# State space: the closing addition of the soft-plus goes from VectorE to ScalarE and GpSimd

## The reference, cut to what matters

```python
dt = jax.nn.softplus(jnp.einsum('blr,rd->bld', dt_r, W_dt) + b_dt)
A = -jnp.exp(A_log)
def step(h, inp):
    dt_t, B_t, C_t, u_t = inp
    dA = jnp.exp(dt_t[:, :, None] * A)
    h = h * dA + dt_t[:, :, None] * B_t[:, None, :] * u_t[:, :, None]
    y = jnp.einsum('bdn,bn->bd', h, C_t)
    return (h, y)
```

## Time and profile before

| what | us |
|---|---|
| median of 3 runs | 1926.7 |
| the profiled execution, first to last instruction (span) | 1948.6 |
| VectorE busy in the span | 1491.3 (77%) |
| TensorE busy | 1562.9 (80%) |
| ScalarE busy | 953.5 (49%) |
| GpSimd busy | 920.7 (47%) |
| state space, from 700 to 1290 us of the span | 590 |
| VectorE busy there | 540.35 |
| GpSimd busy there | 410.72 |
| ScalarE busy there | 365.03 |
| TensorE busy there | 469.73 |

### The profile page before, as it was taken

How to read it: one execution, slowest core, us unless ns; L and a number is a source line. 1 busy time by engine, 2 the same in 40 slices (tenths; PEclk the granted TensorE clock), 3 DMA queues, 4 the chain that set the end, 5 groups by cost and what they waited for, 6 DMA issues and landing times. The chain is left out here.

```text
span 1948.6 us, 31799 instructions
## 1 busy us (share of the span) xinstructions
PE 1562.9 (80%) x10219; PEld 1017.4 (52%) x10219; DVE 1491.3 (77%) x2947; ACT 953.5 (49%) x1491; POOL 920.7 (47%) x938
## 2 busy tenths in 40 slices
PE   8889888989699978977878878769998811699991
PEld 4545547988476632322333333236776611588891
DVE  6899986887488779999989999967777678533335
ACT  3545543575544567657656666436566410011114
POOL 4455442444200147677676677654344100366653
PEclk8999998999899989999988999979999855799996
DMA  4000000000000000000000000020000040466654
GB/s 144 2 0 0 0 1 27 2 2 1 12 1 0 1 1 1 1 1 0 0 1 0 0 0 1 1 78 11 5 9 5 3 145 0 159 209 206 212 171 135
DMA packets 49075, 75.34 MB, mean 39 GB/s; under 512 B 8861, under 2 KB 34821, under 8 KB 48437
## 3 DMA queue, kind: packets, MB, share of 16 engines
q1 hardware_dynamic: 43541, 64.12, 10.5%
q0 software_dynamic: 4544, 9.32, 1.6%
q10 hardware_dynamic: 864, 0.33, 0.1%
HBM read 62.26 MB, written 11.48 MB: 38 GB/s over the span
## 5 line engine op out<-in xcount | busy, mean ns | idle before, releaser
L1506 POOL TENSOR_TENSOR m_hC<-m_h,m_Cs 128x512 f32<-128x512 f32 x256 | 328.2, 1287 | 169.2 <-DVE m_h L1680 122.6
L1788 PE MATMUL PS<-m_hC,identf 128*128 128x512 f32 x512 | 296.5, 662 | 100.9 <-POOL m_hC L1506 99.9
L1680 DVE TENSOR_TENSOR_SCAN m_h<-m_dA,PS 128x512 f32<-128x512 f32 x256 | 312.4, 1220 | 11.2
L1788 PEld LDWEIGHTS PS<-m_hC,identf 128*128 128x128 f32 x512 | 93.0, 203 | 236.4 <-POOL m_hC L1506 208.9
L1675 DVE TENSOR_TENSOR PS<-PS,m_DU 128x512 f32<-128x512 f32 x256 | 178.4, 697 | 19.9 <-issue 3.8
L1616 ACT ACTIVATE m_dA<-m_DT,m_A 128x508 f32<-128x508 f32 x256 | 174.3, 714 | 31.3 <-DVE m_DT L1664 31.1
L1996 ACT ACTIVATE e_Sg<-PS 128x512 f32<-128x512 f32 x71 | 42.4, 597 | 223.0 <-PE PS L2238 178.8
L2238 PE MATMUL PS<-e_xT,e_WT 128*128 128x128 f32 x1136 | 143.8, 281 | 4.9 <-DVE e_xT L2146 3.4
L1608 ACT COPY m_Cs<-PS 128x512 f32<-128x512 f32 x128 | 73.7, 576 | 143.7 <-PE PS L1766 143.5
L2238 PEld LDWEIGHTS PS<-e_xT,e_WT 128*128 128x128 f32 x1136 | 135.4, 195 | 9.3 <-DVE e_xT L2146 7.1
L1935 POOL DMA_INDIRECT e_XG<-token_rows,e_ids x71 | 68.8, 969 | 138.9 <-DVE e_ids L2140 117.6
(11 more groups left out here) (411 smaller groups left out, 3801.6 us busy)
## 6 DMA issues: line engine op xcount, KB each, us to landing
e_WT<-in_w_wgu SPq DMA_DIRECT2D x71, 512.0 KB
token_rows<-X SPq DMA_DIRECT2D x2, 2048.0 KB
e_Y<-expert_rows SPq DMA_DIRECT2D x16, 256.0 KB, 4.0
k_BD<-in_w_bcr SPq DMA_DIRECT2D x1, 2464.0 KB, 9.5
e_w_wd<-in_w_wd SPq DMA_DIRECT2D x1, 2048.0 KB, 7.9
out_dram<-X SPq DMA_DIRECT2D x8, 256.0 KB, 2.4
X<-in_x SPq DMA_DIRECT2D x1, 1792.0 KB, 8.7
x_Cs<-in_ctx SPq DMA_DIRECT2D x8, 154.0 KB
```

The lines of the kernel that those rows point to most:

```text
L1506: nc.gpsimd.tensor_tensor(hC[:, i % ND, :], hst[:, i % ND, :], Cs[:, n % ND, :], ALU.mult).then_inc(s["hC"], 1)
L1680: nc.vector.tensor_tensor_scan(hst[:, i % ND, :], dA[:, i % NA].rearrange("p b l -> p (b l)"), bank(4), 0.0, ALU.mult, ALU.add).then_inc(s ...
L1788: nc.tensor.matmul(bank(5 + ch), c.identf[:, :], hC[:, i % ND, :], start=False, stop=(n == NS - 1)).then_inc(s["yacc"], 1)
```

## The change: what it does

VectorE's instruction L1664 goes away (16 of them, two for each group). ScalarE gets an instruction that rectifies `m_DT` in place, for both halves at once, right behind the absolute value. GpSimd gets two additions for each group, `m_DT` + `m_L`, at slots 26 and 28, and the two products `m_DU` move from slots 28 and 29 to 29 and 30. The counts of the semaphore `ab` are fitted to the fourth step of ScalarE; TensorE's transposition of the next group now waits for the second bias instruction of the group before instead of the absolute value.

```diff
-"z_copy0": 27, "softplus0": 27, "inputs0": 28, "inputs1": 29, "softplus1": 30, "z_copy1": 30, "xn_copy": 31}
+"z_copy0": 27, "softplus0": 26, "softplus1": 28, "inputs0": 29, "inputs1": 30, "z_copy1": 30, "xn_copy": 31}
...
+            def softplus(ch):
+                def stage(g, par):
+                    pool.wait_ge(s["ab"], g * 4 + 4)
+                    pool.wait_ge(s["t"], g * 4 + ch * 2 + 2)
+                    nc.gpsimd.tensor_tensor(DT[:, par, ch, :], DT[:, par, ch, :], L[:, ch, :], ALU.add).then_inc(s["dt"], 1)
+                return stage
...
-                act.wait_ge(s["ab"], g * 3 + 2)
+                act.wait_ge(s["ab"], g * 4 + 2)
                 nc.scalar.activation(L[:, :, :], DT[:, par], ACT.Abs).then_inc(s["ab"], 1)
+                act.wait_ge(s["ab"], g * 4 + 3)
+                nc.scalar.activation(DT[:, par], DT[:, par], ACT.Relu).then_inc(s["ab"], 1)
...
-            def softplus(ch):
-                def stage(g, par):
-                    dve.wait_ge(s["t"], g * 4 + ch * 2 + 2)
-                    nc.vector.scalar_tensor_tensor(DT[:, par, ch, :], DT[:, par, ch, :], 0.0, L[:, ch, :], ALU.max, ALU.add).then_inc(s["dt"], 1)
-                return stage
...
-                    pe.wait_ge(s["ab"], g * 3)
+                    pe.wait_ge(s["ab"], g * 4 - 2)
```

More of the change, by code:

```diff
@@ L1435, in state_space @@
             "mids": 22, "z0": 22, "dt_bias": 24, "corrected0": 24, "low": 25, "exps": 25, "corrected1": 25, "z1": 25, "corrected2": 26, "xn_T": 26,
-            "corrected3": 27, "logs": 27, "z_copy0": 27, "softplus0": 27, "inputs0": 28, "inputs1": 29, "softplus1": 30, "z_copy1": 30, "xn_copy": 31}
+            "corrected3": 27, "logs": 27, "z_copy0": 27, "softplus0": 26, "softplus1": 28, "inputs0": 29, "inputs1": 30, "z_copy1": 30, "xn_copy": 31}
     OPEN = {"inner_stats": 4, "inner_rstd": 6, "inner_norm": 7, "xn_T": 7, "xn_copy": 7, "x0": 7, "x1": 8, "x2": 8, "x3": 8, "silus": 9, "dt_b_c": 9, "parts": 10,
@@ L1518, in _ @@
             early = {"inner_rstd": inner_norm}
-            prepare = {"corrected0": corrected(0, 0), "corrected1": corrected(0, 1), "corrected2": corrected(1, 0), "corrected3": corrected(1, 1), "inputs0": inputs(0), "inputs1": inputs(1)}
+            prepare = {"corrected0": corrected(0, 0), "corrected1": corrected(0, 1), "corrected2": corrected(1, 0), "corrected3": corrected(1, 1), "softplus0": softplus(0), "softplus1": softplus(1), "inputs0": inputs(0), "inputs1": inputs(1)}
             setup()
@@ L1592, in exps @@
                     nc.scalar.preload_act_table_set("natural_log_exp_and_others")
-                act.wait_ge(s["ab"], g * 3 + 3)
+                act.wait_ge(s["ab"], g * 4 + 3)
                 nc.scalar.activation(E1[:, :, :], L[:, :, :], ACT.Exp, scale=-1.0).then_inc(s["e"], 1)
@@ L1692, in _ @@
             early = {"inner_stats": stats}
-            prepare = {"rest": rest, "last": last, "softplus0": softplus(0), "softplus1": softplus(1)}
+            prepare = {"rest": rest, "last": last}
             setup()
@@ L1718, in stage @@
                     if ch == 0:
-                        pe.wait_ge(s["ab"], g * 3 + 1)
+                        pe.wait_ge(s["ab"], g * 4 + 1)
                     else:
```

## The result

| | kernel before | changed kernel |
|---|---|---|
| median, 5 runs each, us | 1927.0 (1926.4 to 1931.3) | 1945.8 (1941.9 to 1951.2) |
| ratio to the kernel before | | 1.0096, 95% interval 1.0083 to 1.0109 |

The changed kernel is 18.8 us slower; 15.7 were forecast. In the two traces the state space alone accounts for it: the last gate begins at 1306.29 us of the span, where it was 1287.98, 18.3 us later. The profiled execution of the changed kernel has a span of 1941.4 us and a time of its own of 1943.3; the trace of the kernel before is of an execution 21.9 us over its median, and what is longer there lies behind the state space (from the last gate to the end of the span 660.7 us, against 635.1 in the changed kernel). So the traces are compared over the state space only.

What follows compares the result with a forecast made beforehand. GpSimd's queue at each hand-over was taken as the bound once changed (VectorE before). Seven hand-overs, 12.9 us, plus 2.8 for group 0 made 15.7 us slower: 1926.7 becomes 1942.4, said as 1942, range 1933 to 1951.

Steps and rivals of the forecast that it cites:

- The bound: Hand-over: GpSimd's queue, now 15 operations to step 31's product, sets the gate, about 19.6 us after the first correction.
- The Relu: ScalarE's rectifying instruction, ahead of the whole chain: the first correction on GpSimd starts 1.09 us later.
- The additions: GpSimd's queue in the hand-over: each addition costs 1.22 us, and the 0.45 us stretch beside L1664 goes.
- Full or half clock at the gate: TensorE's last pair, seven hand-overs: 10.1 us longer at the full clock, 15.7 at the half; the middle, 12.9, taken.
- The opening: Ahead of group 0: additions in GpSimd's queue and ScalarE's 1.09 us make VectorE's first product 2.8 us later.
- The step that failed: From a gate to the next first correction: follows VectorE's steps and ScalarE's queue; no cost there beyond ScalarE's 1.09 us.
- if the time goes to TensorE in the middle of a group: Middle of a group: a listed sign that the forecast is wrong; no size given.
- The third rival: Behind hand-overs: TensorE stays at the half clock into the next group, 10 to 15 us on top, about 1955; chance 0.10.

Runs made afterwards that it cites:

- Run 8: Run 1's kernel with GpSimd's two additions on 4 of the 512 columns: 1920.8 us.
- Run 3: The changed kernel with the second addition and the two products `m_DU` one slot earlier on GpSimd: 1946.9 us.
- run 11: The changed kernel with added TensorE matmuls at the hand-over and in steps 5 to 7 behind the gate: 1937.8 us.
- run 1: The changed kernel with ScalarE's Relu moved behind the last instruction of its chain, additions still on GpSimd: 1937.9 us.
- run 2: The changed kernel with the maximum and the addition back on VectorE, so only the Relu in ScalarE's chain is new: 1929.3 us.
- run 10: Run 2's kernel with added TensorE matmuls at the hand-over and in steps 5 to 7 behind the gate: 1926.6 us.
- run 9: Run 1's kernel with added TensorE matmuls at the hand-over and in steps 5 to 7 behind the gate: 1927.5 us.
- run 4: The changed kernel with four added TensorE matmuls in each of the steps 28 to 31 at the hand-over: 1947.5 us.
- run 5: The changed kernel with three added TensorE matmuls in each of the steps 5 to 7, ahead of the x projection: 1941.1 us.
- run 7: The kernel before with added TensorE matmuls at the hand-over and in steps 5 to 7 behind the gate: 1921.2 us.
- run 12: Run 7's kernel without the four added matmuls at step 30: 1916.6 us.

## Why the prediction was right

**The bound.** That GpSimd's queue in the hand-over decides, and not its idle time over a group, held: 19.64 us in six of seven hand-overs, with the 15th operation 17.15 us after the first. Run 8 shows it: shorter additions give 17.2 us. Run 3, `m_DU` earlier, gives nothing, as it should by this.

**The Relu.** 1.09 us for each group were taken, and 7 x 1.09 is what the stretches from gate to correction show (run 11: 7.7), and about what run 1 gave back (7.9 with the opening). What I had not seen is that the kernel before can absorb this: its gates had TensorE's half clock in six of seven, and with the later chain they had it in two (run 2). Alone the Relu cost 1.3 us.

**The additions.** 1.22 us each, with the stretch of 0.45 us gone, as the rule on the shared ports in the Trainium skill ("SBUF — State Buffer", section "SBUF: two separate sides") would have it: no preparing operation of GpSimd shown above is longer than 1.27 us now that L1664 is gone. ("1.27 elsewhere" was read from the hand-over alone; the earlier trace rows have a 1.59 at 704.46, there too beside an L1664.) The runs bear it out: in the kernel before and in runs 2 and 10, where VectorE has the instruction, two of GpSimd's operations in every hand-over take 1.71 to 1.74 us; in the changed kernel and in runs 1, 9 and 11 none takes over 1.35. On GpSimd in run 2:

```profile
844.29 1.72 POOL L1488 TENSOR_TENSOR m_E<-m_E 128x512 f32<-128x512 f32 x1
```

In run 8 the price by itself was 17.2 us, against the 14.4 of 2.05 x 7 and about 1 at the opening; run 1's gates at the half clock are in it.

**Full or half clock at the gate.** I took the middle, 12.9. This term was too large, by 2.3: 7.6 for the Relu and 3.0 from correction to gate make 10.6, close to the 10.1 of the full clock, because the pair for step 31 was at the full clock in six of seven. Half-clock pairs stand ahead of it (1.95 and 1.67 us at 780.28 and 782.74), and cost nothing there, as GpSimd's pace of 2.45 us for each product covers them.

**The opening.** 2.8 us forecast, 2.4 between the two traces: 1.7 on GpSimd as worked out, and 0.7 at the first correction. The Relu is there nearly in full, though: ScalarE's chain starts at its bias instruction, before and then changed

```profile
691.20 1.26 ACT L1586 ACTIVATE m_DT<-PS,w_bdt 128x512 f32<-128x512 f32 x2
```

```profile
690.95 1.26 ACT L1593 ACTIVATE m_DT<-PS,w_bdt 128x512 f32<-128x512 f32 x2
```

and the first correction follows 9.32 and 10.27 us behind it, 0.95 later. The other 0.25 us is the stage before, which ended earlier in this trace.

**The step that failed** is the one that priced the rest of a group at nothing. The prediction had "if the time goes to TensorE in the middle of a group" among the signs of being wrong, and 5.9 of the 18.3 us went there. The third rival (TensorE stays at the half clock into the next group, 10 to 15 us, about 1955) was given 0.10, and a smaller form of it came true in four groups: not as slow steps, but as an x projection that is late for ScalarE and VectorE some eight steps on. Its reason was wrong: TensorE does not stay at the half clock. In the changed kernel its granted clock is 1.00 for the first 15 us behind each of the gates of groups 0 to 5, and falls again behind that; more work at the hand-over leaves this as it is (run 4), and work just ahead of the projection takes 4.7 us away (run 5, by the medians).

What the half clock costs at this place can be read from groups 1, 3 and 5, which take the same time in every trace where the clock is full. In the 14 traces these are 42 stretches from a gate to the next first correction; 1.09 us is taken off where the Relu is in the chain:

| granted clock 17 to 23 us behind the gate | stretches | us |
|---|---|---|
| 0.82 to 1.00, and full behind that | 22 | 52.5 to 52.7 |
| 1.00, but 0.94 from 23 to 52 us | 5 | 53.3 to 53.4 |
| 0.72 | 5 | 53.6 to 53.9 |
| 0.57 to 0.60 | 10 | 54.0 to 54.3 |

All three groups of the kernel before are in the first line. Of the changed kernel group 1 has 0.72 and group 3 has 0.58; with both sets of matmuls (run 11) all three are at 1.00, and the excess is gone. In groups 2 and 6 the clock there went from 0.75 to 0.50 and from 1.00 to 0.75; in group 4 it is 0.50 in both kernels, and that group is longer by the Relu alone. So the 5.9 us are, by these rows, the price of the half clock at the x projection. Why it falls there more often in the changed kernel stays open.

The sum: 15.7 forecast, less 2.3 for the clock at the gate, less 0.4 at the opening, less 0.6 between the last two gates, and 5.9 more in the groups: 18.3 in the trace, 18.8 by the medians. The misses have opposite signs, so that the total came within 3 us of the forecast is in part luck.

## What to carry to other kernels

An engine that is half idle over a stage can be the bound where the work lands: count the operations in its queue from the event that releases them to the event that somebody waits for, and multiply. An instruction on the path of a chain can cost its full length there, and nothing a few instructions later: the same Relu behind the chain gave 7.9 us back. Whether it does depends on what else is late: alone it cost 1.3 us on the kernel before. Where the granted clock changes from kernel to kernel, price a part of a change with the clock held, or its cost is mixed with that of TensorE's clock.

## What the runs showed of the hardware

- 16 bf16 matmuls a group that nobody reads, placed where TensorE waits for GpSimd, and 9 more behind the gate, raised the granted clock of the state space from 0.94 to 0.97 on the kernel before, and took 6.5 us off (run 7). Without the four that stood ahead of a pair the clock is lower, 0.95, and the time too: 11.6 us less than the kernel before (run 12). So the mean clock of a stage does not tell the time here; where in the group the half clock falls does.
- With work in one place the half clock moves rather than goes: with work added only ahead of the x projection it came at the gate (run 5), with work added only at the gate it stayed at the projection (run 4). With both, groups 1, 3 and 5 have the full clock from gate to gate (run 7).
- A GpSimd operation on 4 columns took 0.19 us, the same on 512 columns 1.27, and 1.22 from one start to the next in a row.
- A GpSimd operation of 1.27 us took 1.71 to 1.74 beside VectorE's `scalar_tensor_tensor` with two inputs in SBUF, twice in every hand-over of three kernels, and never in the four looked at without it.
